# GpSimd's order at the start of a four-layer attention kernel: ones and query moves ahead of two memsets, register keys moved by SP, layer 0's weights in two loads

## The chip, the cores and the metric

The kernel runs on one core of a Trainium2 chip. The core has TensorE (PE, matmuls), VectorE (DVE), ScalarE (ACT), GpSimd (POOL) and SyncE (SP), each with its own instruction stream, and 16 DMA engines that serve the queues of SP, ACT and GpSimd. The metric is the device time of one execution in microseconds; lower is better.

## The reference

The input x has 16 x 16 places with 192 channels. Four attention layers are added to it one after the other, each on a group-normalised copy. Every layer has 12 heads of 16 channels over 256 places.

```python
x = x + L0(_gn(x))   # attention with relative position bias: q.Rh[row] + q.Rw[col]
x = x + L1(_gn(x))   # layer norm, rotary q and k, a bias per head, then a feed-forward block of 768
x = x + L2(_gn(x))   # 7 x 7 neighbourhood mask, and 16 register tokens as extra keys and values
x = x + L3(_gn(x))   # as L0
...
attn = softmax(q @ k.T * scale + bias);  out = (attn @ v) @ proj_w + proj_b
```

## The kernel before, in words

All activations stay in SBUF, channels on partitions, 96 channels in each of two chunks (NC = 2). Each engine has a stream written out by hand, with semaphores between them; nothing reorders it. `wait_ge` blocks the whole stream of its engine.

For the scores, queries and keys are stacked on partitions: QS[0] and QS[1] (layers 0 and 2, and 1 and 3) hold for each of the 12 heads 16 high query rows, 16 low query rows, the high rows again, and four blocks of bias or mask rows (ROW_HIGH, COL_HIGH, ROW_LOW, COL_LOW); KS holds the matching key rows, with 16 register columns in front and behind. A single 128-row matmul then gives a product of nearly full precision with the bias in it. Rows get into the stacks by small DMAs from SBUF to SBUF (`rows_of`), which is how this kernel moves data between partitions. The four first partitions of QS carry minus the maxima, and those of KS a one per head, loaded from `ones`.

A layer runs: group norm (`squares`, `stats_psum`, XN), projections, the split into high and low parts (QHL, KH, KL), in layers 0 and 3 the relative terms (ROWH, ROWL, COLH, COLL), the moves into QS and KS, and then on TensorE `for_maxima(l, h)` (L995), `turn_maxima` (L1009), `scores` (L1031), `values` (L1056) in a fixed interleaving, and `out_project` (L1066). The wait for the moves of the first heads stands ahead of head 0 ("q stack", "k stack", "first rows"); heads 4 and 8 wait for the second and third groups in layers 0 and 3, head 6 for the moves of the upper six heads in every layer ("later heads", "later keys").

Who moves what around the change: in layer 0 SP moves group 0's queries, keys and row terms, and the later row terms; GpSimd scales the key columns of w0 (L412), sets five backgrounds (VX, twice NM, ONESC, VR, L421), waits for the hot rows (the one-hot key rows, copied from HOT into KS by ACT, L538, and DVE, L843), loads `ones` (L425), and moves groups 1 and 2 of the queries (L455, L458), group 0's low row terms (L464) and all column terms (L441). Then it writes layer 1's bias rows (L485) and scales later weights. In layer 1 GpSimd moves the first six heads' low queries (L430) and high keys (L433), adds the rotated part to the second chunk of QF (L504), makes QL of it (L506), moves layer 2's register keys (L513, twelve moves of 6 KB) and layer 2's mask rows (L516, four of 192 KB). SP moves the rest (L329), ACT the high keys (L586).

`keep_warm(bank, n)` (L917) runs n matmuls on a tile of zeros whose result nobody reads. `project` (L935) and L1138, L1144 are projections; `loaded(pe, "w0")` is the wait for layer 0's weights, one load of 576 KB.

## Time and profile before

| | us |
|---|---|
| median of 3 runs | 158.56 |
| lowest, highest | 157.37, 159.72 |
| profiled execution, time | 159.08 |
| profiled execution, span from first to last instruction | 156.4 |
| TensorE busy | 141.6 (91% of the span) |
| VectorE busy | 91.1 (58%) |
| ScalarE busy | 70.7 (45%) |
| GpSimd busy | 53.1 (34%) |

Times in views are microseconds from the start of the span. The profiled execution is one more execution beside the three. TensorE's busy share holds warming matmuls too, and it is an average over stages: at the places of the change TensorE waits. Times of views with "issue" are times in which an engine waited for nothing that the profile shows.

### The profile page before, as it was taken

Reading aid. Unit: us, or ns where it says so; the run is one execution under the profiler, and the core shown is the slowest. Engines: PE = TensorE matmul, PEld = TensorE weight load, DVE = VectorE, ACT = ScalarE, POOL = GpSimd, SP = SyncE. Lnnn points to the kernel's source line nnn. Section 1 sums busy time; section 2 is a strip of 40 time slices with the busy share of each in tenths; the row PEclk is TensorE's granted clock in tenths of the full one; section 3 lists DMA queues with packets and bytes.
Section 4 is the critical chain, followed back from the end, with each engine's and each line's share of the span. In section 5 each row is a group of like instructions: output and inputs, shape, how many; then the busy total and the mean of one; then the engine's idle time right before and its main releaser. Section 6 shows DMA issues by size and latency. Waiting matters only on the chain.

```text
span 156.4 us, 2663 instructions
## 1 busy us (share of the span) xinstructions
PE 141.6 (91%) x920; PEld 94.2 (60%) x920; DVE 91.1 (58%) x239; ACT 70.7 (45%) x164; POOL 53.1 (34%) x94
## 2 busy tenths in 40 slices
PE   6989589999898958999999999968999999999992
PEld 2569366645457836755458865756666478676550
DVE  2775368736734988876541026666634845697462
ACT  4474127761233216682137713417571445167810
POOL 7689988840200289930000000720000047600000
PEclk9999999999999999999999999999999999999999
DMA  3907648999200156820000000450000017620001
GB/s 84 260 19 184 196 123 262 275 295 298 64 2 0 51 168 96 169 41 0 4 0 0 0 0 2 146 156 4 0 0 0 0 49 212 171 82 0 0 0 50
DMA packets 12508, 13.55 MB, mean 87 GB/s; under 512 B 4144, under 2 KB 10336, under 8 KB 12496
## 3 DMA queue, kind: packets, MB, share of 16 engines
q1 hardware_dynamic: 7792, 9.29, 21.0%
q0 software_dynamic: 3472, 3.01, 8.6%
q10 hardware_dynamic: 1232, 1.08, 2.4%
q8 instruction: 7, 0.11, 0.3%
q14 instruction: 5, 0.04, 0.1%
HBM read 6.82 MB, written 0.20 MB: 45 GB/s over the span
## 4 chain that ended last, share of the span: by engine, by line
PE 62%; DMA 9%; POOL 7%; ACT 7%; DVE 6%; issue 4%; SPq 3%; DVEq 0%; POOLq 0%; ACTq 0%
PE PC L1056 14%; PE RING L1031 9%; PE RING L917 4%; PE RING L995 4%; DMA KS<-KL 4%; PE PA L1066 4%; PE RING L1260 3%; DMA WQKV<-in_w 3%; PE PB L1066 3%; PE PB L995 2%; ACT PR L634 2%; DMA QS<-COLL 2%; SPq L329 2%; PE PA L1266 2%; PE PB L1266 1%
## 5 line engine op out<-in xcount | busy, mean ns | idle before, releaser
L634 ACT ACTIVATE PR<-RING 128x512 f32<-128x512 f32 (+1 forms) x48 | 25.7, 553 | 9.3 <-PE RING L1031 9.1
L917 PE MATMUL RING<-WARM 128*128 128x512 bf16 x84 | 24.7, 406 | 1.3 <-POOL WARM L388 1.3
L1056 PE MATMUL PC<-PR,VX 128*32 128x256 f32 (+1 forms) x192 | 23.6, 369 | 0.1
L827 DVE TENSOR_REDUCE NM<-RING 128x2 fp32r<-128x512 f32 (+1 forms) x32 | 20.1, 652 | 4.1 <-PE RING L995 3.9
L1031 PE MATMUL RING<-QS,KS 128*128 128x256 f32 (+1 forms) x96 | 20.2, 305 | 0.3 <-ACT QS L626 0.2
L1031 PEld LDWEIGHTS RING<-QS,KS 128*128 128x128 f32 x96 | 13.9, 188 | 7.7 <-issue 4.5
L626 ACT ACTIVATE QS<-PA 4x512 fp32r<-4x512 f32 (+1 forms) x20 | 10.6, 531 | 16.5 <-PE PA L1009 16.5
L430 POOL DMA_DIRECT2D QS<-QL x2 | 1.1, 550 | 43.0 <-DVE QL L778 31.0
L827 DVE TENSOR_REDUCE NM<-PB 128x2 fp32r<-128x512 f32 (+1 forms) x16 | 10.5, 654 | 5.6 <-PE PB L995 5.5
L1056 PEld LDWEIGHTS PC<-PR,VX 128*32 128x32 f32 x192 | 8.6, 109 | 8.4 <-ACT PR L634 1.8
L995 PE MATMUL RING<-KS,QS 128*128 128x256 f32 (+1 forms) x64 | 13.2, 298 | 0.0
L917 PEld LDWEIGHTS RING<-WARM 128*128 128x128 bf16 x84 | 8.3, 111 | 7.7 <-issue 1.6
L834 DVE STREAM_TRANSPOSE TURNED_U<-PC 128x256 f32<-128x256 f32 x12 | 5.4, 450 | 12.8 <-PE PC L1056 12.8
L995 PE MATMUL PB<-KS,QS 128*128 128x256 f32 (+1 forms) x32 | 7.3, 308 | 5.9 <-DMA QS<-COLL 2.7
L455 POOL DMA_DIRECT2D QS<-QHL x8 | 4.1, 516 | 24.8 <-ACT QHL L609 24.8
L995 PEld LDWEIGHTS RING<-KS,QS 128*128 128x128 f32 x64 | 9.4, 189 | 2.0 <-DVE NM L827 1.2
L995 PEld LDWEIGHTS PB<-KS,QS 128*128 128x128 f32 x32 | 5.0, 189 | 8.9 <-issue 7.2
L553 ACT ACTIVATE SQUARED<-X 96x256 f32<-96x256 f32 x8 | 3.3, 414 | 12.3 <-DVE X L890 7.9
L412 POOL TENSOR_SCALAR WQKV<-WQKV 96x384 f32<-96x384 f32 x4 | 5.3, 1324 | 9.7 <-DMA WQKV<-in_w 9.6
L1066 PE MATMUL PA<-O,WO 128*96 128x256 f32 x24 | 7.8, 405 | 0.0
L1066 PE MATMUL PB<-O,WO 128*96 128x256 f32 x24 | 7.1, 379 | 0.0
L485 POOL TENSOR_SCALAR QS<-HOT,ABS 128x256 fp32r<-128x256 f32 x12 | 6.7, 555 | 1.2
(189 smaller groups left out, 271.6 us busy)
## 6 DMA issues: line engine op xcount, KB each, us to landing
WQKV<-in_w SPq DMA_DIRECT2D x2, 576.0 KB, 8.5
WO<-in_wo SPq DMA_DIRECT2D x4, 288.0 KB, 8.8
W<-in_ff SPq DMA_DIRECT2D x2, 576.0 KB, 9.6
KS<-KH ACTq DMA_DIRECT2D x10, 96.0 KB, 3.1
WQKV<-in_w SPq DMA_DIRECT2D x2, 432.0 KB, 5.3
QS<-QHL POOLq DMA_DIRECT2D x12, 64.0 KB, 2.6
KS<-KL SPq DMA_DIRECT2D x8, 96.0 KB, 3.1
QS<-QH SPq DMA_DIRECT2D x8, 96.0 KB, 2.3
```

What stands on the lines that cost most here:

```text
L412: g.tensor_scalar(w[:, :, first:first + C], w[:, :, first:first + C], QK_SCALE, None, ALU.mult)\
L485: g.tensor_scalar(QS[1][:, h, :], HOT[:, :], ABS[:, 2, h:h + 1], ABS[:, 1, h:h + 1], ALU.mult, ALU.add).then_inc(sem("ab rows"), 1)
L626: A(QS[l % 2][0:GH, heads[0]:heads[-1] + 1, :], turn_bank(t)[0:GH, None, 0:T].to_broadcast([GH, len(heads), T]), ACT.Copy).then_inc(sem("m ...
L634: A(PR[:, h % NPR, 0:n], exponents(l, h)[:, 0:n], ACT.Exp).then_inc(sem("probs"), 1)
L827: V.tensor_reduce(NM[:, TURN_OF[h], :, h % GH], MAXIMA[h % 3][:, 0:2 * n_keys].rearrange("p (q k) -> p q k", q=2), AX.X, ALU.max, negate=T ...
L834: link(V.transpose(TURNED_U[:, :, :].rearrange("p b r -> p (b r)"), PC[g % 2][:, 0:T]))
L917: M(bank, WARM[:, 0:P], WARM[:, :], start=True, stop=True)
L995: ins = M(s[:, q * n_keys:(q + 1) * n_keys], QS[l % 2][:, h, q * P:(q + 1) * P], KS[:, h, keys], start=True, stop=True)
L1031: ins = M(half(s, l, k), KS[:, h, KEY0 + k * P:KEY0 + (k + 1) * P], QS[l % 2][:, h, reach(l, k)], start=True, stop=True)
L1056: ins = M(columns(h)[:, reach(l, k)], VX[:, k, h, :], half(PR[:, h % NPR, :], l, k), start=(k == 0 and l != 2), stop=(k == 1), skip_group_ ...
L1066: ins = M(y_psum(m), WO[l][:, g, m * CC:(m + 1) * CC], in_order(O[g][:, :]) if l in REL_LAYERS else O[g][:, :], start=(g == 0), stop=(g == ...
L1260: ins = M(s[:, i * T:(i + 1) * T], W1[:, k, c * P:(c + 1) * P], XN[:, k, :], start=(k == 0), stop=(k == NC - 1))
```

## The change

In words, part by part:

- GpSimd loads `ones` directly after the scaling of w0 and the wait for the hot rows, then sets VX and NM, and then starts on the query moves. ONESC and VR are set after layer 0's column terms.
- The hot rows are split 4 heads to ACT and 8 to DVE, before 6 and 6.
- Layer 0's weights come in two loads of 288 KB: query columns (w0q) ahead of vecs, and key and value columns where w0 stood. TensorE waits for w0q ahead of the query matmuls, and for w0 ahead of the keys. GpSimd's scaling waits for w0, now the second load.
- TensorE runs 5 warming matmuls in place of 7 ahead of layer 0's statistics, and none in place of 1 between the two.
- In layer 1 SP moves the low queries of the first six heads; GpSimd did. SP also moves the twelve register key pieces, behind its last move of layer 1, and waits for "kr parts" ahead of them.

GpSimd's stream at the start of layer 0, before. NM are zeros for the maxima, VX the values' tile, QHL the split queries.

```order
L412 TENSOR_SCALAR WQKV<-WQKV 96x2x192
L421 MEMSET VX 128x768
L421 MEMSET NM 128x192 x2
L421 MEMSET ONESC 96x96
L421 MEMSET VR 128x384
L425 DMA KS<-in_ones 4x12x272
L455 DMA QS<-QHL 16x4x256 x2
L458 DMA QS<-QHL 16x4x256
```

The same place now:

```order
L420 TENSOR_SCALAR WQKV<-WQKV 96x2x192
L427 DMA KS<-in_ones 4x12x272
L430 MEMSET VX 128x768
L430 MEMSET NM 128x192 x2
L466 DMA QS<-QHL 16x4x256 x2
L469 DMA QS<-QHL 16x4x256
L466 DMA QS<-QHL 16x4x256 x2
L469 DMA QS<-QHL 16x4x256
```

The load of ones moved ahead of the memsets, and two memsets left this place; they stand behind the last COLL move now.

GpSimd's stream in layer 1, before. QL, KH are low queries and high keys of a chunk, KRH and KRL the register keys.

```order
L430 DMA QS<-QL 16x6x256
L433 DMA KS<-KH 16x6x256
L504 TENSOR_TENSOR QF<-QF,RFq 48x256
L506 TENSOR_TENSOR QL<-QF,QH 96x256
L513 DMA KS<-KRH 16x6x16 x4
L513 DMA KS<-KRL 16x6x16 x2
L513 DMA KS<-KRH 16x6x16 x4
L513 DMA KS<-KRL 16x6x16 x2
L516 DMA QS<-in_mask 16x12x256 x4
```

The same place now:

```order
L444 DMA KS<-KH 16x6x256
L517 TENSOR_TENSOR QF<-QF,RFq 48x256
L519 TENSOR_TENSOR QL<-QF,QH 96x256
L523 DMA QS<-in_mask 16x12x256 x4
L459 MEMSET QS 4x3072
```

The four mask moves now stand directly behind QL, with no register keys ahead of them.

SP's stream in layer 1, as a difference (the rows without a sign are in both; in_w0q and the other loads stand far ahead of this):

```order
 L329 DMA QS<-QH 16x6x256 x2
+L329 DMA QS<-QL 16x6x256
 L329 DMA KS<-KL 16x6x256
 L329 DMA QS<-QH 16x6x256 x2
 L329 DMA QS<-QL 16x6x256
 L329 DMA KS<-KL 16x6x256
+L348 DMA KS<-KRH 16x6x16 x4
+L348 DMA KS<-KRL 16x6x16 x2
+L348 DMA KS<-KRH 16x6x16 x4
+L348 DMA KS<-KRL 16x6x16 x2
```

SP has one move more ahead of the first KL, and the twelve register moves behind the last.

```diff
@@ -67,7 +67,7 @@
     [f"bk{l}" for l in range(LAYERS)] + ["bkp"]
     + [f"{v}{l}" for l in range(LAYERS) for v in ("bq", "bo")] + ["bqp", "ln1g", "ln1b", "ln3g", "ln3b", "b2"])}
 
-HOT_HALF = NH // 2
+HOT_HALF = NH // 3
 SCALED = ("w0", "w2", "w1", "wp", "w3")
 
 def build(nc, a, out):
@@ -262,7 +262,7 @@
         def slot(*use):
             return RINGS[RING_OF[use[0]]][number[use] % 2]
 
-        loads = [("x", X, "xT"), ("gavg", GAVG, "gavg"), ("vecs", VECS, "vecs"), ("w0", WQKV[0], "w0"), ("hot", HOT, "hot"),
+        loads = [("x", X, "xT"), ("gavg", GAVG, "gavg"), ("w0q", WQKV[0][:, :, 0:Q2], "w0q"), ("vecs", VECS, "vecs"), ("w0", WQKV[0][:, :, Q2:Q2 + 2 * C], "w0"), ("hot", HOT, "hot"),
                  ("qbias", QBIAS, "qbias"), ("relt", RELT, "relt"), ("vb0", VB[:, 0, :], "vb0"), ("pcol", PCOL, "pcol"), ("abt", ABT, "abt")]
         later_loads = [
                  ("wo0", WO[0], "wo0"), ("vb", VB[:, 1:LAYERS, :], "vb"), ("w2", WQKV[2], "w2"), ("regt", REGT, "regt"), ("w1", WQKV[1], "w1"), ("wp", WP, "wp"),
@@ -282,11 +282,11 @@
         signals |= {"q psum": {0: NG, 1: NC, 2: NC, 3: NG}, "k psum": {l: NC for l in range(LAYERS)},
                     "turned": {1: 4 * NC}, "qf": {1: NC}, "kf": {1: NC},
                     "qh": {0: NG, 1: NC, 2: NC, 3: NG}, "ql": {0: NG, 1: NC, 2: NC, 3: NG},
-                    "q stack": {l: (5 if l in REL_LAYERS else 2) * 16 for l in range(LAYERS)},
+                    "q stack": {0: 5 * 16, 1: 3 * 16, 2: 2 * 16, 3: 5 * 16},
                     "k stack": {l: (3 if l in REL_LAYERS else 2) * 16 for l in range(LAYERS)},
                     "later heads": {l: (1 if l in REL_LAYERS else 4) * 16 for l in range(LAYERS)}}
         signals |= {"later keys": {l: 2 * 16 for l in range(LAYERS)},
-                    "first rows": {l: (4 if l in REL_LAYERS else 2) * 16 for l in range(LAYERS)}}
+                    "first rows": {0: 4 * 16, 1: 16, 2: 2 * 16, 3: 4 * 16}}
         signals |= {"x": {l: 3 * NC if l == 1 else NC for l in range(LAYERS)}, "sums": {0: 1}}
         signals |= {name: {l: count for l in REL_LAYERS} for name, count in {
             "rel psum": 4, "rel h": len(REL_PARTS), "rel l": len(REL_PARTS), "second heads": 4 * 16, "third heads": 4 * 16,
@@ -336,9 +336,17 @@
                         heads = slice(i * HPC, (i + 1) * HPC)
                         for block in (Q_HIGH, Q_AGAIN):
                             move("qh", rows_of(queries, block)[:, heads], QH[:, i, :], "later heads" if i else "q stack", i + 1)
-                        if i:
-                            move("ql", rows_of(queries, Q_LOW)[:, heads], QL[:, i, :], "later heads", i + 1)
+                        if i or l == 1:
+                            move("ql", rows_of(queries, Q_LOW)[:, heads], QL[:, i, :], "later heads" if i else "q stack", i + 1)
                         move("kl", rows_of(KS, Q_AGAIN, KEY0, REG1)[:, heads], KL[:, i, :], "later heads" if i else "k stack", i + 1)
+                    if l == 1:
+
+                        sync.wait_ge(sem("kr parts"), 2)
+                        for col in (0, REG1):
+                            for block, src in ((Q_HIGH, KRH), (Q_LOW, KRH), (Q_AGAIN, KRL)):
+                                for i in range(NC):
+                                    sync.dma_start(rows_of(KS, block, col, col + NREG)[:, i * HPC:(i + 1) * HPC].bitcast(F32), src[:, i, :].bitcast(F32))\
+                                        .then_inc(sem("kr stack"), 16)
                     continue
 
                 def move_group(signal, block, src, g, count):
@@ -415,20 +423,23 @@
 
             scale_keys("w0", WQKV[0], Q2)
 
-            for n, (tile, value) in enumerate((
-                    (VX[:, :, :, :], 1.0), (NM[:, 0:3].bitcast(F32), 0.0),
-                    (NM[:, 3:6].bitcast(F32), 0.0), (ONESC[:, :], 1.0 / C), (VR[:, :, :], 0.0))):
-                g.memset(tile, value).then_inc(sem("backgrounds"), 1)
-                pool.wait_ge(sem("backgrounds"), n + 1)
-
             pool.wait_ge(sem("hot rows"), 2)
             pool.dma_start(KS[0:GH, :, KEY0:REG1 + NREG], a["ones"]).then_inc(sem("one rows"), 16)
 
+            def background(n, tile, value):
+                g.memset(tile, value).then_inc(sem("backgrounds"), 1)
+                pool.wait_ge(sem("backgrounds"), n)
+
+            background(1, VX[:, :, :, :], 1.0)
+            background(2, NM[:, 0:3].bitcast(F32), 0.0)
+            background(3, NM[:, 3:6].bitcast(F32), 0.0)
+
             def move_first_rows(l):
 
-                pool.wait_ge(*upto("ql", l, 1))
-                pool.dma_start(rows_of(QS[l % 2], Q_LOW)[:, 0:HPC].bitcast(F32), QL[:, 0, :].bitcast(F32))\
-                    .then_inc(sem("first rows"), 16)
+                if l == 2:
+                    pool.wait_ge(*upto("ql", l, 1))
+                    pool.dma_start(rows_of(QS[l % 2], Q_LOW)[:, 0:HPC].bitcast(F32), QL[:, 0, :].bitcast(F32))\
+                        .then_inc(sem("first rows"), 16)
                 pool.wait_ge(*upto("kh", l, 1))
                 pool.dma_start(rows_of(KS, Q_LOW, KEY0, REG1)[:, 0:HPC].bitcast(F32), KH[:, 0, :].bitcast(F32))\
                     .then_inc(sem("first rows"), 16)
@@ -469,6 +480,8 @@
                     move_first_rows(2)
                 if l == 0:
 
+                    background(4, ONESC[:, :], 1.0 / C)
+                    background(5, VR[:, :, :], 0.0)
                     loaded(pool, "abt", "pcol", "hot")
                     g.tensor_scalar(ABH[:, :, :], ABT[:, :, :], 1.0, None, ALU.mult).then_inc(sem("ab cols"), 1)
                     pool.wait_ge(sem("ab cols"), 1)
@@ -506,12 +519,6 @@
                     g.tensor_tensor(QL[:, 1, :], QF[:, 1, :], QH[:, 1, :].bitcast(F32), ALU.subtract).then_inc(sem("ql"), 1)
 
                     pool.wait_ge(*upto("scores", 0, NH))
-                    pool.wait_ge(sem("kr parts"), 2)
-                    for col in (0, REG1):
-                        for block, src in ((Q_HIGH, KRH), (Q_LOW, KRH), (Q_AGAIN, KRL)):
-                            for i in range(NC):
-                                pool.dma_start(rows_of(KS, block, col, col + NREG)[:, i * HPC:(i + 1) * HPC], src[:, i, :])\
-                                    .then_inc(sem("kr stack"), 16)
                     for block in (ROW_HIGH, COL_HIGH, ROW_LOW, COL_LOW):
                         pool.dma_start(rows_of(QS[0], block), a["mask"][FREE + block:P:BLOCKS, None, :].to_broadcast([HD, NH, T]))\
                             .then_inc(sem("mask rows"), 16)
@@ -1108,7 +1115,7 @@
                 free = RINGS[0][0][:, :]
                 if l:
                     pe.wait_ge(*upto("probs", l - 1, max(AFTER_MAXIMA) + 1))
-                keep_warm(free, (7, 3, 3, 3)[l])
+                keep_warm(free, (5, 3, 3, 3)[l])
                 if l == 0:
                     loaded(pe, "gavg")
                 for i in range(NC):
@@ -1118,7 +1125,7 @@
                         pe.wait_ge(*upto("x", l - 1, signals["x"][l - 1] - NC + i + 1))
                     pe.wait_ge(*upto("squares", l, i + 1))
                     M(stats_psum(i), GAVG[:, :], SUMS[:, i, :], start=True, stop=True).then_inc(sem("gstats"), 1)
-                    if i == 0:
+                    if i == 0 and l:
                         keep_warm(free, 1)
                 keep_warm(free, 2 if l == 1 else 7)
                 if l == 1:
@@ -1130,7 +1137,7 @@
                     layer_norm(1, free, *ready)
                     register_keys()
                     ready = upto("ni", 1, NC)
-                loaded(pe, f"w{l}")
+                loaded(pe, f"w{l}" if l else "w0q")
                 if l in REL_LAYERS:
                     for k in range(NC):
                         chunk_ready(*ready, k)
@@ -1143,6 +1150,7 @@
                     for k in range(NC):
                         ins = M(thirds, WQKV[l][:, k, 2 * P:3 * P], by_parity(XN[:, k, :]), start=(k == 0), stop=(k == NC - 1))
                     ins.then_inc(sem("q psum"), 1)
+                    loaded(pe, f"w{l}")
                     pe.wait_ge(sem("k scaled"), 2 + SCALED.index(f"w{l}"))
                     project(chunk_psum("k", l, 0), WQKV[l], Q2, *ready).then_inc(sem("k psum"), 1)
                 else:
@@ -1378,6 +1386,7 @@
     for l in range(LAYERS):
         arrays[f"w{l}"] = chunks(wqkv[l])
         arrays[f"wo{l}"] = by_quadrant(wo[l])
+    arrays["w0q"], arrays["w0"] = arrays["w0"][:, :, 0:Q2], arrays["w0"][:, :, Q2:]
     return {name: np.ascontiguousarray(v, dtype=f32) for name, v in arrays.items()}
 
 def kernel(**inputs):
```

## Rows read from the trace of the kernel before

**Rows 1.** The page, chain of work that ended last, shares of the span by engine.

```profile
PE 62%; DMA 9%; POOL 7%; ACT 7%; DVE 6%; issue 4%; SPq 3%; DVEq 0%; POOLq 0%; ACTq 0%
```

**Rows 2.** The chain, pieces in order of time, 0 to 24: start, length, what.

```profile
1.65 0.43 SPq L322
...
7.17 1.81 POOL WQKV L412
...
10.45 0.17 POOL ONESC L421
...
10.68 0.43 POOL VR L421
11.11 0.30 issue
11.41 0.79 POOL KS L425
...
16.74 3.26 DMA QS<-COLL
```

**Rows 3.** Timeline of TensorE, 0 to 22.5: start, busy, line, operation, count.

```profile
1.31 3.17 PE L917 MATMUL RING<-WARM 128*128 128x512 bf16 x7 [1.31 <-POOL WARM L388]
...
5.12 1.88 PE L917 MATMUL RING<-WARM 128*128 128x512 bf16 x7
7.06 0.70 PE L1138 MATMUL PA<-XN,WQKV 96*128 96x256 f32 x2
...
20.23 0.48 PE L995 MATMUL PB<-KS,QS 128*128 128x256 f32 x2 [2.42 <-DMA QS<-COLL]
```

**Rows 4.** Timeline of DVE and ACT, 6.9 to 9.

```profile
7.03 0.41 DVE L720 TENSOR_SCALAR XN<-X,GM,GT 96x256 f32<-96x256 f32 x1
...
7.34 1.48 ACT L538 ACTIVATE KS<-HOT 128x1536 fp32r<-128x1536 f32 x1 [1.19 <-DMA HOT<-in_hot]
...
7.41 1.20 DVE L843 CAST KS<-HOT 128x1536 fp32r<-128x1536 f32 x1
```

**Rows 5.** The chain, pieces in order of time, 54 to 62.

```profile
58.18 3.01 DMA KS<-KL
```

**Rows 6.** Timeline of all engines, 50 to 72, the rows of layer 1's moves.

```profile
53.91 0.56 SPq L329 DMA_DIRECT2D KS<-KL  x1
...
53.95 0.56 POOL L430 DMA_DIRECT2D QS<-QL  x1 [11.96 <-DVE QL L772]
54.32 0.47 DVE L763 SCALAR_TENSOR_TENSOR RFq<-PC,VECS,ROPE 48x256 f32<-48x256 f32 x1
...
55.06 0.74 POOL L504 TENSOR_TENSOR QF<-QF,RFq 48x256 f32<-48x256 f32 x1
...
56.99 2.04 POOL L513 DMA_DIRECT2D KS<-KRH  x4
...
57.21 0.47 PE L995 MATMUL PB<-KS,QS 128*128 128x256 f32 x2 [1.63 <-DMA KS<-KH]
...
61.28 0.47 PE L995 MATMUL PB<-KS,QS 128*128 128x256 f32 x2 [0.57 <-DMA KS<-KL]
...
63.05 2.17 POOL L516 DMA_DIRECT2D QS<-in_mask  x4
```

**Rows 7.** DMA queues (q1 SP, q10 ACT, q0 GpSimd): 58.2 to 60.2; 60.2 to 61.4; 63.6 to 64.6; 65.6 to 66.6.

```profile
q1 hardware_dynamic: 324, 0.29, 50.6%
q0 software_dynamic: 381, 0.02, 29.0%
q10 hardware_dynamic: 165, 0.14, 23.6%
...
q1 hardware_dynamic: 12, 0.01, 1.5%
...
GB/s 0 41 54 19 29 44 23 18 5 0 0 0 0 0 0 0 0 0 0 0 0 0 0 0 0 0 0 0 0 82 861 123 123 205 205 287 246 287 410 205
...
q0 software_dynamic: 323, 0.31, 133.7%
```

## The prediction

> **What bounds the kernel now.** I read the chain of work that ended last first, then its pieces in order of time over the two places that the change touches, then the timeline there. TensorE carries 62% of the chain, DMA 9% and GpSimd 7% [rows 1]. The change touches almost nothing on TensorE, so what it can move lies in the small shares: the start of layer 0, where the chain runs over GpSimd and a transfer, and the start of layer 1, where it runs over SP and a transfer. Both are places where TensorE stands still and waits for data.
>
> Layer 0: the chain is the load of w0, then GpSimd alone: key scaling from 7.17 to 8.98, five memsets, the load of ones at 11.41, the query moves from 11.41 + 0.79 = 12.20, and at last the first group's low column terms, issued at 16.74 and landed 3.26 later [rows 2]. The first maximum matmul starts at 20.23 after 2.42 us of waiting for that transfer [rows 3]. GpSimd issues one move right behind the other from 11.41 on, so its queue is the limit, and what goes from in front of it comes off the start of the attention one for one, down to about 17.8, where TensorE's own work ends (20.23 less 2.42).
>
> Layer 1: head 0 starts at 57.21 after 1.63 us of waiting for GpSimd's key move, but this is given back: the chain does not end there. Head 6 starts at 61.28 and waits 0.57 us for the last key-low move, which SP issued at 58.18 and which took 3.01 [rows 5, 6]. So head 6 is the wait that sets layer 1, and head 0 is not.
>
> **Part 1, GpSimd in layer 0: two memsets leave the queue's front.** ONESC costs 0.17 and VR 0.43; with a step of 0.05 behind each (10.45 + 0.17 to 10.68) that is 0.70. Between the last memset and the first DMA lie 0.30 of issue [rows 2]. In the new order a compute instruction stands before a DMA twice (key scaling before ones, NM before the query moves). If the 0.30 is paid twice the gain is 0.70 - 0.25 = 0.45; if the step costs 0.05 both times, it is 0.70 + 0.25 = 0.95. The row that exists is 0.30 for a memset before a DMA, so one 0.30 and something between for the other: I take 0.6. The two memsets come back after the column terms, in front of the bias rows of layer 1. That costs the bias rows 0.70 - 0.6, about 0.1 us, well ahead of layer 1 in time: nothing.
>
> **Part 2, the new gate in front of the ones.** Its DMA, and behind it everything that GpSimd does, waits for both halves of the hot rows. Before, ACT took 6 heads in 1.48 (7.34 to 8.82) and DVE 6 in 1.20 (7.41 to 8.61) [rows 4], both under the key scaling. Now DVE has 8 heads: 1.20 x 8/6 = 1.60, so it ends at 9.01, 0.03 after the key scaling. Cost 0.05. This cover is now gone: each 0.1 us that HOT lands later costs GpSimd 0.1. HOT is issued one SP issue later (0.43 [rows 2], about 0.47 with the step to the next); if the landing follows in full, GpSimd loses 0.45 of its 0.6. I take no delay, because HOT landed close behind w0 (ACT started on it at 7.34, GpSimd on w0 at 7.17) and the same bytes stand before it as before: the engines were busy with w0 then, not waiting for an issue. For ACT the smaller half is a gain: 1.48 x 4/6 = 1.0, the table's high part RELH, next on ACT, starts some 0.4 earlier, and with it the high and low query parts, about 0.3. SP's moves start 0.3 earlier by that; they are not last at 20.23.
>
> **Part 3, w0 in two loads.** The queries' half takes the place of vecs in the issue order, so its bytes can start 0.47 earlier, and the rest is issued 0.47 later than w0 was. The query matmuls started at 7.06 [rows 3], as w0 landed, but their second chunk needs XN, which DVE finished at 7.03 + 0.41 = 7.44 [rows 4]; they gain some 0.4, and their reader, ACT, is busy with hot rows until then, so it lies under part 2. For the end only the second half counts, since key scaling waits for it. Landing bounds: 0.4 earlier to 0.47 later. I take 0.
>
> **Part 4, three warming matmuls fewer.** Seven take 3.17 from 1.31, 453 ns each, so the seventh ends at 4.48 [rows 3]; five end near 3.6, and the sums, not the warming, then set the start. The statistics start about 0.25 earlier, and XN with them. It is off GpSimd's path: 0.
>
> Layer 0 in sum: -0.6 + 0.05 + 0 + 0 = **-0.55**, bounds -1.3 (0.95 and the early landing) and +0.3 (0.45, and both loads late).
>
> **Part 5, layer 1's first low query move goes from GpSimd to SP.** GpSimd loses one issue of 0.56 at 53.95, so the key move behind it can go about 0.5 earlier, and head 0 gains about 0.4. SP takes it in between the high queries and the key-low move of 53.91, which it hardly delays, since SP waits there for DVE anyway. What counts for head 6 is the add on QF at 55.06: it also needs the rotated part that DVE has ready at 54.32 + 0.47 = 54.79 [rows 6]. So it starts at about 54.85: 0.2 earlier, no more. QH, SP's four moves and the key-low move follow 0.2 earlier, issued at 57.98.
>
> **Part 6, the register keys go to SP, and the mask rows come forward.** In the kernel before GpSimd spent 56.99 to 63.05 on twelve small moves, and only then issued the four mask moves [rows 6]. Now the twelve stand on SP behind the last key-low move, where SP has nothing to do until layer 2: twelve times 0.6 is 7 us from 58.6, hidden. But GpSimd now issues the four mask moves at about 57.0, into the transfers on which head 6 waits. No row shows this; two rows bound it. In the two us from 58.2, SP's queue moved 0.29 MB and ACT's 0.14, with only 0.02 of GpSimd's between, and the key-low move took 3.01 [rows 5, 7]. The mask alone fills the engines, 0.31 MB per us [rows 7], and it is 4 x 192 KB. Its first bytes came 1.3 after its first issue (63.05, [rows 6]), in slice 30 of 40 from 63.6, at 64.3 [rows 7]; here that is 58.2 or just after. If the three queues take turns, then from 58.2 on SP's remaining 0.27 MB (0.29 + 0.01 before, less what moves in the 0.2 us of the earlier start) get 0.10 per us while ACT has its last 0.12 (1.2 us), then half of 0.31: 0.15 / 0.155 = 1.0. The last bytes move near 60.4; before it was about 60.2, after which SP's queue had only 0.01 MB [rows 7]. So taking turns costs 0.0 to 0.3. If the transfers go in order of issue, some 0.58 MB of mask stand in front of the last key-low move; at 0.31 from about 57.4 on, 1.3 after SP's first issue, (0.48 + 0.58 + 0.10) / 0.31 = 3.7 gives 61.1 and, with the 1.0 between last bytes (60.2) and landing (61.19), 62.1 to 62.4: 0.9 to 1.2 later than 61.19. Below zero: if the mask cost nothing and the twelve small moves (29% of the engines' time in these 2 us) were gone, the landing would be 0.5 earlier. I take turns, because the row shows all three queues moving in the same 2 us, none waiting for the other: head 6 at 61.5, **+0.2** instead of the -0.2 that part 5 alone would give. From head 6 on TensorE works in order, so the layer shifts by it.
>
> The Trainium skill, "DMA: Bandwidth & Descriptors", section "Queues, rings and completion order", says that each engine goes round robin between queues, a whole packet of descriptors at a time. This speaks against the order-of-issue price and for +0.2; by the same page's rule that all issuers share the same 16 engines the mask is not free either. The row with three queues active agrees.
>
> **Sum.** -0.55 + 0.2 = -0.35, with rounding -0.4. The profiled execution took 159.08 (span 156.4, 2.7 around it), which makes 158.7. It was 0.5 above the median of the three runs, so against the median of 158.56 the forecast is **158.2**. The three runs spread over 157.37 to 159.72; 2% is 3.2 us, about what a measurement of this kernel can tell from no change.
>
> **The rivals.**
> A, slower: the mask moves delay head 6. It decides as soon as the key-low move lands more than 0.55 later than in the profile before, after 61.75. In order of issue it is +1.0, up to +1.4 if all of the mask goes first: 158.56 - 0.55 + 1.0 = 159.0, at most 159.4. For it: the engines are at nine tenths there already. Against: the queues take turns in the row. Chance 0.20.
> B, layer 0 gains nothing: HOT or the second half of w0 lands an SP issue later, hot rows end at 9.5, GpSimd gains 0.15, and layer 1 gives +0.2: 158.6. That is also what the change would be if it did not do what it says, since its query moves would then leave when they did. For it: 288 KB in shorter rows, one issue more in front. Chance 0.12.
> C, both ends good: 0.95 in layer 0, and no collision, -0.5 in layer 1: 158.56 - 1.45 = 157.1. For it: the small moves that leave the critical 2 us. Against: 0.30 has been seen. Chance 0.15.
> D, TensorE's clock: the first seven warming matmuls took 453 ns each, the later seven 269 [rows 3], the step from 1.2 to 2.4 GHz. With three fewer and a pause of some 0.5 us before the sums it may rise later. The query matmuls, of which a pair takes 0.70 or less [rows 3], then take up to twice as long: six pairs, between 0 and some 3 us. GpSimd's queue covers part of it; I take +1.0 on the start of layer 0 in place of the -0.55, with layer 1's 0.2: 159.8. Against: in the profile longer pauses (2.42 us before 20.23) leave the clock granted full. Chance 0.05. The Trainium skill, "TensorE: Matmul & The Clock Gate", section on the HAM clock gate, says that the array starts throttled and that activity releases it; the rows agree with the first half.
>
> **How the numbers follow.** The forecast, 158.2 with its own range of 157.6 to 158.7, has 0.48; A 0.20, C 0.15, B 0.12, D 0.05. From C, less the spread of a median of few runs, to the upper end of A; D lies above it: 156.9 to 159.5. No case leaves the 2% band; what is left for either side is what I have not seen: 0.04 faster, 0.92 same, 0.04 slower.
>
> **What the changed profile would show.** Right: GpSimd's first query move at 11.6 instead of 12.20, the first maximum at 19.7, its wait still for COLL; head 6 of layer 1 waiting longer than 0.57 for the key-low move, which takes 3.3 to 3.6. Wrong: the ones after 9.5 (B), a landing over 4 us (A), query matmuls of 12% to 100% longer (D), a head 6 without a wait (C). The forecast is also wrong if the start of layer 0 moves earlier and head 4 or 6 there takes up the wait, behind the later groups' moves, or if layer 2's start moves though nothing there was changed.

## The result, and the profile after

| | before | after |
|---|---|---|
| median, us | 158.86 (4 runs, 157.37 to 159.72) | 163.44 (4 runs, 162.85 to 165.16) |
| ratio, 95% interval | | 1.032, 1.020 to 1.043 |
| profiled execution, us (its span) | 159.08 (156.4) | 165.16 (163.4) |

The change makes the kernel 3% slower, 4.6 us. The forecast was 158.2, with a range of 156.9 to 159.5. Medians here and below hold all runs; the ratios leave out runs over 1.5% above the fastest of their kernel, which leaves e4 without a ratio. Lines of the code are some 7 further down after the change: L995 is now L1002, L1138 is L1145, L1031 is L1038.

The page of the changed kernel, the chain by engine and by line, is the first hint: TensorE's share is down from 62% [rows 1] and DMA's is up from 9%, and key-low moves alone have 6%.

```profile
PE 59%; DMA 12%; DVE 8%; POOL 7%; ACT 6%; issue 4%; SPq 3%; DVEq 0%; POOLq 0%; ACTq 0%
PE PC L1063 14%; PE RING L1038 9%; DMA KS<-KL 6%; PE RING L1002 4%; PE PA L1073 4%; PE RING L924 4%; DMA QS<-COLL 3%; PE RING L1268 3%; DMA WQKV<-in_w 3%; PE PB L1002 3%; PE PB L1073 3%; SPq L329 2%; PE PA L1274 2%; PE PB L1274 2%; DVE NM L834 2%
```

The chain of the changed kernel in order of time over layer 1's start (start, length, what) shows which one:

```profile
58.33 6.03 DMA KS<-KL
```

It was issued at 58.33, before at 58.18, and took 6.03 us instead of 3.01 [rows 5]. Head 6 starts at 64.45 instead of 61.28. The timeline of the changed kernel there has both sides of it: GpSimd's mask moves are issued from 1.4 us ahead of SP's last key-low move on, and TensorE waits 3.95 where it waited 0.57 [rows 6].

```profile
55.03 0.72 POOL L517 TENSOR_TENSOR QF<-QF,RFq 48x256 f32<-48x256 f32 x1 [0.25 <-DVE RFq L770]
...
56.95 2.18 POOL L523 DMA_DIRECT2D QS<-in_mask  x4
...
57.00 0.47 PE L1002 MATMUL PB<-KS,QS 128*128 128x256 f32 x2 [1.26 <-DMA KS<-KL]
...
57.47 0.82 SPq L329 DMA_DIRECT2D QS<-QL  x1
...
58.33 0.65 SPq L329 DMA_DIRECT2D KS<-KL  x1
...
59.03 2.52 SPq L348 DMA_DIRECT2D KS<-KRH  x4
...
64.45 0.77 PE L1002 MATMUL PB<-KS,QS 128*128 128x256 f32 x2 [3.95 <-DMA KS<-KL]
...
65.90 1.07 PE L1063 MATMUL PC<-PR,VX 128*32 128x256 f32 x4
```

The DMA view of the changed kernel, packets, MB and share of 16 engines by queue, once for 58.2 to 60.2 and once for 60.2 to 62.2, says who had the engines. In the first two us SP's queue (q1) got 0.12 MB where it had 0.29 before [rows 7], and GpSimd's (q0) got twice that; in the next two, 2.7 times that.

```profile
q0 software_dynamic: 253, 0.24, 53.0%
q10 hardware_dynamic: 147, 0.13, 26.0%
q1 hardware_dynamic: 137, 0.12, 21.5%
...
q0 software_dynamic: 421, 0.40, 84.9%
q1 hardware_dynamic: 172, 0.15, 32.3%
q10 hardware_dynamic: 76, 0.06, 11.3%
```

Head 6 is 3.17 us late, but layer 1's end (the first sums of the next norm, 76.12 before and 81.97 after) is 5.85 late. The windows view of the changed kernel (length, busy time and count by engine, then the granted clock, DMA share, GB/s) has the other 2.7: TensorE stands still for the pause, and for 6.8 us behind it runs at about half clock (0.52 granted), that is at 1.2 GHz. Four value matmuls then take 1.07 us, against 0.63 at full clock. In the kernel before, the clock is full from 58 to 76.

```profile
58.00:61.30 3.30, 2.45 (x17) 1.85 (x15) 3.19 (x6) 1.84 (x4) 3.30 (x4) 1.00 0.99 249
61.30:64.20 2.90, 0.00 (x0) 0.00 (x0) 0.00 (x0) 0.00 (x0) 0.43 (x1) 0.95 0.99 171
64.20:71.00 6.80, 6.55 (x28) 4.42 (x29) 2.77 (x5) 2.31 (x4) 0.00 (x0) 0.52 0.07 8
71.00:76.00 5.00, 5.00 (x42) 2.98 (x40) 4.09 (x14) 4.25 (x9) 0.00 (x0) 1.00 0.00 0
```

Layer 0 gave nothing in this execution: the first maximum stands at 20.71, before at 20.23. The chain of the changed kernel there: the second w0 load lands at 7.58, the step behind the scaling is 0.42, the step behind NM 0.29, and the query moves leave at 12.58, not at 11.6 (before: 12.20).

```profile
3.02 4.56 DMA WQKV<-in_w
...
7.73 1.95 POOL WQKV L420
9.68 0.42 issue
10.10 0.79 POOL KS L427
...
12.28 0.29 issue
12.58 1.03 POOL QS L466 x2
...
17.12 3.35 DMA QS<-COLL
20.47 0.24 issue
20.71 0.48 PE PB L1002 x2
```

A last loss stands where nothing was changed: in layer 3, head 4 waits 1.29 us, where before it did not wait. The view names DVE's maxima, but those that head 4 needs were done; what came last is a move of ROWL by SP, issued at 140.2, which took 4.1 us to land, when no such move took over 3.0 before. Timeline of the changed kernel, then its view of ROWL moves from 120 us on:

```profile
144.38 0.47 PE L1002 MATMUL RING<-KS,QS 128*128 128x256 f32 x2 [1.29 <-DVE NM L834]
```

```profile
DMA to landing us min/median/max: 1.8/2.3/4.1
```

### The profile page after: what moved, and what is told of

Same layout as the page of the kernel before. It is cut to its first block, busy times and chain, and to the rows that moved or that the text cites. A ratio compares the mean times of both kernels' runs of the same rounds, so it can differ in the third digit from the quotient of the medians.

```text
span 163.4 us, 2651 instructions
## 1 busy us (share of the span) xinstructions
PE 144.6 (89%) x909; PEld 96.2 (59%) x917; DVE 91.4 (56%) x239; ACT 70.5 (43%) x164; POOL 46.6 (29%) x81
## 4 chain that ended last, share of the span: by engine, by line
PE 59%; DMA 12%; DVE 8%; POOL 7%; ACT 6%; issue 4%; SPq 3%; DVEq 0%; POOLq 0%; ACTq 0%
PE PC L1063 14%; PE RING L1038 9%; DMA KS<-KL 6%; PE RING L1002 4%; PE PA L1073 4%; PE RING L924 4%; DMA QS<-COLL 3%; PE RING L1268 3%; DMA WQKV<-in_w 3%; PE PB L1002 3%; PE PB L1073 3%; SPq L329 2%; PE PA L1274 2%; PE PB L1274 2%; DVE NM L834 2%
## 5 line engine op out<-in xcount | busy, mean ns | idle before, releaser
L1063 PE MATMUL PC<-PR,VX 128*32 128x256 f32 (+1 forms) x192 | 24.5, 379 | 0.1
L924 PE MATMUL RING<-WARM 128*128 128x512 bf16 x74 | 22.8, 420 | 1.6 <-POOL WARM L396 1.3
L1038 PE MATMUL RING<-QS,KS 128*128 128x256 f32 (+1 forms) x96 | 20.7, 311 | 0.4 <-ACT QS L633 0.2
L1038 PEld LDWEIGHTS RING<-QS,KS 128*128 128x128 f32 x96 | 14.4, 195 | 8.2 <-issue 5.1
L1002 PE MATMUL PB<-KS,QS 128*128 128x256 f32 (+1 forms) x32 | 7.8, 328 | 8.7 <-DMA KS<-KL 6.2
L1002 PE MATMUL RING<-KS,QS 128*128 128x256 f32 (+1 forms) x64 | 13.9, 310 | 1.3 <-DVE NM L834 1.3
L441 POOL DMA_DIRECT2D QS<-QL x1 | 0.5, 536 | 43.1 <-DVE QL L785 43.1
L1002 PEld LDWEIGHTS PB<-KS,QS 128*128 128x128 f32 x32 | 5.4, 206 | 11.7 <-issue 10.7
L1002 PEld LDWEIGHTS RING<-KS,QS 128*128 128x128 f32 x64 | 10.1, 202 | 3.5 <-DVE NM L834 3.1
L420 POOL TENSOR_SCALAR WQKV<-WQKV 96x384 f32<-96x384 f32 x4 | 5.4, 1358 | 11.8 <-DMA WQKV<-in_w 11.6
```

The costliest lines, as they stand in the source:

```text
L420: g.tensor_scalar(w[:, :, first:first + C], w[:, :, first:first + C], QK_SCALE, None, ALU.mult)\
L924: M(bank, WARM[:, 0:P], WARM[:, :], start=True, stop=True)
L1002: ins = M(s[:, q * n_keys:(q + 1) * n_keys], QS[l % 2][:, h, q * P:(q + 1) * P], KS[:, h, keys], start=True, stop=True)
L1038: ins = M(half(s, l, k), KS[:, h, KEY0 + k * P:KEY0 + (k + 1) * P], QS[l % 2][:, h, reach(l, k)], start=True, stop=True)
L1063: ins = M(columns(h)[:, reach(l, k)], VX[:, k, h, :], half(PR[:, h % NPR, :], l, k), start=(k == 0 and l != 2), stop=(k == 1), skip_group_ ...
```

## The experiments

The kernel before, run beside them each time, had medians of 158.67 (e1 to e4), 158.64 (e5 to e9), 159.02 (e10 to e13) and 158.98 (e14 to e17). Each run's profile is one execution.

**e1, the masks held back.**

```diff
+                    pool.wait_ge(*upto("later heads", 1, 4 * 16))
                     for block in (ROW_HIGH, COL_HIGH, ROW_LOW, COL_LOW):
```

> The changed kernel, but GpSimd waits for the upper six heads' moves of layer 1 (later heads) before it issues the four mask moves; all else as changed. Theory M (the mask moves in front of head 6 cost the time: 3.95 us of waiting for the last key-low move against 0.57, and behind the pause a lower TensorE clock): the key-low move takes about 3 us again, head 6 waits under 0.6 us, the clock stays granted, and the time is 158.5 to 160. Theory S (the start of layer 0 costs it: one load more, three warming matmuls fewer): unchanged within 1 us of the changed kernel, 162.5 to 164.

Measured: 159.47, ratio 1.005 (0.998 to 1.012). Timeline of e1: the key-low move issued at 58.64 landed in 2.2 us, head 6 started at 60.93 without a wait, and head 0 within 0.4 of where it was. This one wait takes back 3.8 of the 4.6 us (the 0.8 left lies within the interval), so the mask's place is the cause. The twelve register moves are still on SP here: they are not. With them gone from GpSimd's queue the landing is even 0.8 shorter than the 3.01 of before, which e10 and e11, where they stay on it, have too (3.0).

```profile
57.41 0.47 PE L1003 MATMUL PB<-KS,QS 128*128 128x256 f32 x2 [1.37 <-DMA KS<-KL]
...
58.64 0.61 SPq L329 DMA_DIRECT2D KS<-KL  x1
...
61.42 2.17 POOL L524 DMA_DIRECT2D QS<-in_mask  x4 [4.14 <-PE RING L1039]
```

**e2, only the twelve register moves put on SP,** in the kernel before; the mask rows come forward by that.

```diff
+                        sync.wait_ge(sem("kr parts"), 2)
...
+                                    sync.dma_start(rows_of(KS, block, col, col + NREG)[:, i * HPC:(i + 1) * HPC].bitcast(F32), src[:, i, :].bitcast(F32))\
...
-                    pool.wait_ge(sem("kr parts"), 2)
...
-                                pool.dma_start(rows_of(KS, block, col, col + NREG)[:, i * HPC:(i + 1) * HPC], src[:, i, :])\
```

> The kernel before, and of the change only the twelve register key moves put on SP, so that GpSimd's mask moves come forward by 6 us. Theory M: the key-low move takes 5 to 6 us, head 6 waits 3 to 4 us, and the time is 3 to 4.5 us over the kernel before, 162 to 163. Theory S: no change, 158 to 159.5.

Measured: 162.77, ratio 1.022 (1.013 to 1.030). The key-low move took 4.85 us, and head 6 waited for it:

```profile
58.02 0.47 PE L997 MATMUL PB<-KS,QS 128*128 128x256 f32 x2 [1.60 <-DMA KS<-KH]
63.95 0.47 PE L997 MATMUL PB<-KS,QS 128*128 128x256 f32 x2 [2.44 <-DMA KS<-KL]
```

This part alone brings most of the loss. In its profiled execution (163.78) the clock was at half for 3.4 us here too, from 65.4 on.

**e3 and e4, the start of layer 0 undone:** the warming matmuls back to 7 and 1 (e3), w0 in one load again (e4), each in the changed kernel.

```diff
-                keep_warm(free, (5, 3, 3, 3)[l])
+                keep_warm(free, (7, 3, 3, 3)[l])
-                    if i == 0 and l:
+                    if i == 0:
```

```diff
-        loads = [..., ("w0q", WQKV[0][:, :, 0:Q2], "w0q"), ("vecs", VECS, "vecs"), ("w0", WQKV[0][:, :, Q2:Q2 + 2 * C], "w0"), ...
+        loads = [..., ("vecs", VECS, "vecs"), ("w0", WQKV[0], "w0"), ...
```

> The changed kernel with the three warming matmuls of layer 0 put back (7 and 1). Theory M: the start of layer 0 gives back at most 0.5 us, 163 to 163.5, and head 6 of layer 1 waits as in the changed kernel. Theory S: if the clock that rose at 9.3 us in place of 5.8 is what costs, 159 to 161.

> The changed kernel with layer 0's weights in one load again, in its old place in the order. Theory M: key scaling starts at 7.2 in place of 7.7, the first maximum of layer 0 about 0.5 us earlier, 162.7 to 163.4. Theory S: if the second load is what costs, 159 to 161.

Measured: e3 165.5, ratio 1.038 (1.029 to 1.047); e4 165.59. The first matmul of full-clock length starts at 5.0 in e3, as before at 5.8, and at 9.3 in the changed kernel (read from the matmuls' lengths; the granted clock of the windows view is 1.00 there all the way). The time is not better, so neither brings the loss; the key-low move took 5.5 and 5.8 us in them. A few tenths stay possible: in e3's trace the clock was at 0.66 from 21 to 26, where the changed kernel had 1.00, which would hide a small gain, and e12 below undoes both at once and comes out 0.7% under e1, inside both intervals. In e4 w0 was issued at 2.11 and landed in 4.92, at 7.03, as in the kernel before, 0.55 earlier than in the changed kernel. That is one pair of traces: with two loads the key scaling began at 7.15 (e3) to 7.96 in seven kernels, with one load at 7.12 to 7.34 in eleven, so the second load costs it some 0.4 us in the mean and nothing in e3.

**e5, the clock held up in the pause:** 16 warming matmuls ahead of head 6 of layer 1.

```diff
+                if h == HPC and l == 1:
+                    keep_warm(s[:, :], 16)
```

> The changed kernel with 16 warming matmuls (some 3.5 us at full clock) on TensorE ahead of head 6's wait in layer 1. It parts the wait from what follows it. Theory W+C (the wait of about 4 us costs about 3, and the lower clock behind it another 2 to 2.5): the wait for the key-low move stays near 6 us from issue, the clock stays granted behind it, and the time is 1.5 to 2.5 us below the changed kernel, near 161 to 162. Theory W (the wait alone costs, the clock is small): within 0.7 us of the changed kernel.

Measured: 162.56, ratio 1.022 (1.017 to 1.028). Timeline and windows of e5: head 6 is as late as in the changed kernel (64.36), but the clock behind it stays full.

```profile
60.70 3.63 PE L924 MATMUL PB<-WARM 128*128 128x512 bf16 x16
64.36 0.50 PE L1004 MATMUL PB<-KS,QS 128*128 128x256 f32 x2
...
65.20 0.63 PE L1065 MATMUL PC<-PR,VX 128*32 128x256 f32 x4
```

```profile
64.30:71.00 6.70, 6.66 (x51) 4.54 (x52) 4.83 (x9) 4.19 (x9) 0.00 (x0) 1.00 0.06 6
```

e5 is 3.9 over the kernel before, the changed kernel 4.6: the clock is some 0.7 of the medians (1% by the ratios, 2.7 us in the profiled execution; it differs between executions), and with the 0.8 that e1 keeps, the wait itself is 3.1. That the clock fell for the pause is shown; what it costs in the median is not settled, since the intervals of e5 and of the changed kernel overlap.

**e6 and e9, whose bytes they are and on which queue.** Both start from e1. They add four plain loads of the same mask rows into an unused tile DUM, 768 KB; e6 on GpSimd, where the change had the mask moves, e9 on SP directly behind its last key-low move.

```diff
+                        pool.dma_start(rows_of(DUM, block), a["mask"][FREE + block:P:BLOCKS, None, :].to_broadcast([HD, NH, T]))\
```

```diff
+                            sync.dma_start(rows_of(DUM, block), a["mask"][FREE + block:P:BLOCKS, None, :].to_broadcast([HD, NH, T]))\
```

> The mask moves wait for the upper heads' moves as in e1, and at their early place GpSimd issues four plain loads of the same rows, size and shape into a scratch tile that nothing reads (extra work). The mask moves convert float32 to the matmul's rounded float32 on the way, these do not. Theory B (bytes and packets of GpSimd's queue delay the key-low move): it takes 5 to 6 us as in the changed kernel, time 162.5 to 165. Theory K (the conversion is what makes the collision dear): the key-low move takes 3.3 to 4 us, time 159.5 to 161.

> As e6, but SP issues the four plain loads, directly behind its last key-low move, so that they stand in the same queue and behind it, at nearly the same time (from 59). Theory Q (the order in one queue protects what is ahead): the key-low move takes 3 to 3.3 us, head 6 waits under 0.6 us, time as e1, 158.5 to 160. Theory T (all traffic in flight shares the engines alike): the key-low move takes over 4 us, time over 161.

Measured: e6 165.68, ratio 1.046 (1.037 to 1.054), key-low 5.83 us, head 6 waiting 3.64: bytes for an unused tile delay it as the mask rows do. e9 157.81, ratio 0.993 (0.989 to 0.997), key-low 2.2 us, no wait of head 6. The same bytes, 0.7 us behind the key-low move instead of 1.4 ahead of it, cost nothing. Two things differ between e6 and e9, the queue and the moment of issue, and no run parts them: large loads on SP ahead of the key-low move, or on GpSimd's queue right behind it, were not tried. The DMA view of e9, 58 to 62 (issues: KB each, median us to landing):

```profile
q1 hardware_dynamic: 846, 0.78, 60.3%
q10 hardware_dynamic: 175, 0.15, 11.9%
...
DUM<-in_mask SPq DMA_DIRECT2D x4, 192.0 KB, 3.4
...
KS<-KL SPq DMA_DIRECT2D x1, 96.0 KB, 2.2
```

**e7, half of the dose:** two of the four mask moves ahead, two behind the wait of e1.

```diff
+                        if block == ROW_LOW:
+                            pool.wait_ge(*upto("later heads", 1, 4 * 16))
```

> Two of the four mask moves (384 KB) go at the early place, two behind the upper heads' moves. Theory B in proportion: the key-low move takes about 4.4 us in place of 3 or 6, head 6 waits 1.5 to 2.5, and the clock mostly stays; time 160 to 161.5. Theory F (a move behind them waits for whatever was issued before, so the first ones decide): the same as with all four, over 162.5.

Measured: 161.11, ratio 1.012 (1.005 to 1.019). Key-low 4.32 us (2.2 with none of the mask, 6.03 with all of it); head 6 at 62.97, after 2.10 of waiting, and no fall of the clock in its trace. Landing against bytes is near proportional: some 2 us of landing for each 384 KB ahead, of which TensorE feels what is over some 2.3 (3.01 and 0.57 of waiting before, 4.32 and 2.10 here).

```profile
58.56 4.32 DMA KS<-KL
62.97 0.47 PE PB L1004 x2
```

**e10 and e11, the rest of the change by itself.** e10 is the kernel before with GpSimd's new order in layer 0 only; e11 adds the first low query move on SP in layer 1, with the register moves on GpSimd, and the mask behind them, as before.

```diff
-HOT_HALF = NH // 2
+HOT_HALF = NH // 3
+            background(1, VX[:, :, :, :], 1.0)    # behind the ones; ONESC and VR behind COLL
-                        if i:
+                        if i or l == 1:                # e11 only
```

> The kernel before with only GpSimd's new order in layer 0: the hot rows split 4 to 8, ones behind the key scaling, VX and NM, then the query moves, and ONESC and VR behind the column terms. One w0 load, the warming matmuls, and all of layer 1 as before. If the layer 0 part failed through the second load and SP's longer issues, this alone gives 0.3 to 0.5: query moves near 11.8, first maximum near 19.8, 158.0 to 158.4 against 158.6 before. If the issue step in front of a transfer is paid twice and eats it, nothing: first maximum at 20.0 to 20.3, 158.5 to 158.8. Head 6 of layer 1 waits 0.5 to 0.6, as before.

> The one before, plus the move of the first low query part of layer 1 on SP; the twelve register moves stay on GpSimd in front of the masks. Part 5 of the prediction says 0.2 less than the run with the order alone, by the wait of head 6 (0.57 to some 0.4): 157.8 to 158.2. Rival: the move stands on SP's queue in front of the key-low move and delays it by its own issue, so nothing, or 0.1 to 0.3 more. The key-low move should take about 3, not 4 to 6, since no mask bytes stand before it.

Measured: e10 159.2, ratio 0.998 (0.992 to 1.004); e11 158.92, ratio 1.002 (0.998 to 1.007). Neither part changes the time beyond the intervals. The chain of e10:

```profile
7.18 2.06 POOL WQKV L412
9.24 0.41 issue
9.64 0.79 POOL KS L419
...
11.84 0.29 issue
12.13 1.03 POOL QS L457 x2
```

Two memsets (0.70) are gone, but the step in front of a DMA is paid twice, 0.41 and 0.29 for 0.30, and the scaling next to DVE's longer copy took 2.06 for 1.81 [rows 2]: 12.13 against 12.20. The first maximum of e10 still came at 19.53, 0.70 earlier than before, because the COLL move behind it landed in 2.60 instead of 3.26. That landing varies by itself: e12, e14, e15 and e16 are the same program up to there and have 3.73, 2.64, 3.76 and 3.52. A few tenths won on GpSimd are smaller than this spread. In e11 the add on QF starts 0.96 us behind the start of DVE's last QF step and in e10 1.14, so 0.18 is gained, as part 5 says; but the low query move of SP ahead of the key-low move takes 0.82 instead of 0.61, and the key-low move stands 4.26 us behind that DVE step in both (52.95 to 57.21, 54.12 to 58.38).

**e12 and e13, the best of the parts:** e1 with the warming and the one load of before (e12), and with DMA_WARM, the warming matmuls in the pauses ahead of head 0, raised (e13).

```diff
-DMA_WARM = (2, 3, 3, 2)
+DMA_WARM = (10, 7, 8, 2)
```

> The changed kernel with the mask moves held back behind the later heads of layer 1 (as in the first of these runs), the old warming (7 and 1) and one w0 load. What is left of the change: GpSimd's order, QL and the register moves on SP. If the warming and the load explain the 0.8 that the first run stayed above the kernel before, it comes to 157.6 to 158.6. If those 0.8 are the mask's later place or the extra work on SP, it stays at 159 to 159.5. Key-low landing 2 to 2.5, no wait of head 6.

> The same with more warming matmuls while TensorE waits for the moves ahead of head 0 (10, 7, 8 and 2 instead of 2, 3, 3 and 2). If the granted clock falls behind the pause ahead of head 0 of layer 0 (half at 21 to 25 in runs so far) because TensorE stood still there, it stays full now, and the time falls by 0.5 to 1.5 against the run without. If the warming reaches past the landing of the moves, head 0 starts later by up to 1 us and it is a wash.

Measured: e12 159.11, ratio 0.998 (0.992 to 1.004); e13 158.25, ratio 0.999 (0.995 to 1.003). e12 has no wait of head 6, yet gains nothing on the kernel before: head 4 of layer 3 waits, as in the changed kernel and in e1 (timeline of e12; then its ROWL moves from 120 us on):

```profile
138.71 0.47 PE L1003 MATMUL RING<-KS,QS 128*128 128x256 f32 x2 [1.08 <-DVE NM L835]
```

```profile
DMA to landing us min/median/max: 2.0/2.8/3.7
```

e13 kept the clock full in 11 of 12 runs. The kernel before on that chip had it full (0.997 or more) in 10 of 35, with a mean of 157.69, and a mean of 159.29 in the 24 at 0.986 to 0.989. But e13's own 11 average 158.15, so part of that was lost again; by what is not shown.

**e14 to e17, the late move in layer 3.** In every kernel with twelve register moves on SP up to here but e9 and e13 one ROWL move of layer 3 took 3.3 us or more (changed kernel 4.1, e1 4.2, e2 4.0, e3 3.4, e4 3.9, e5 3.3, e6 3.9, e7 3.8, e12 3.7), in before, e10 and e11 none over 3.0, nor in e9, with four more DMAs on SP (2.7). So four (e14) or eight (e15) copies of 6 KB to an unused tile, behind the register moves in e12; e9's four large loads in e12 (e16); and e14 with DMA_WARM of (10, 3, 3, 2) (e17).

```diff
+                        for n in range(4):             # e15: 8
+                            sync.dma_start(rows_of(DUM, Q_HIGH, n * NREG, (n + 1) * NREG)[:, 0:HPC]..., KRH[:, 0, :]...)
```

> e12 (mask late, old warming, one load) with four small copies of 6 KB to an unused tile on SP's queue behind the twelve register moves; result unused. If the number of DMAs on SP's queue sets which one lands late, the slow one leaves the place that head 4 of layer 3 waits for: ROWL at most 3.0 instead of 3.7, no wait of head 4 (e12: 1.08), 0.7 to 1.2 us less than e12, 157.5 to 158.3 against 159 before on the chip of e12. If the number does not matter, it stays as e12: a landing of 3.5 or more and a wait near 1.

> The same with eight small copies. If a periodic event of SP's queue is what is seen, eight put it at another DMA again; no wait of head 4, or a late move at another place (a group of third heads, layer 3's first heads, or a later load), so a time within 0.5 of e14. If more DMAs only give more delay, a longer wait than in e12.

> e12 with e9's four unused loads of 192 KB on SP between its last key-low move and the register moves. The number of DMAs is that of e14. If the number counts, this is as e14 within 0.4, without a wait of head 4 in layer 3, whatever the bytes; e9's result (0.7% faster than the kernel before) repeats. If e9 was chance, it comes out at e12's time or the time before, with a wait of head 4 near 1.

> e14 with ten instead of two warming matmuls in the pause ahead of head 0 of layer 0 alone. In e13 such warming in four layers kept TensorE's clock full in 11 of 12 runs, but full-clock runs were 0.5 us over those of before. With layer 0's alone the clock should stay full in most runs and those 0.5 should go if they came from the other layers' warming: 157 to 157.7, 1% below the kernel before. If the clock falls behind head 0 of layer 1 or 2 instead, it is as e14.

| | median | ratio | longest ROWL | wait of head 4, layer 3 |
|---|---|---|---|---|
| e14 | 158.78 | 0.996 (0.990 to 1.001) | 2.9 | none |
| e15 | 158.03 | 0.994 (0.988 to 0.999) | 3.0 | none |
| e16 | 158.7 | 0.998 (0.992 to 1.005) | 3.0 | none |
| e17 | 157.66 | 0.993 (0.989 to 0.998) | 3.0 | none |

Four, eight and four large ones all take the wait away, and 6 KB copies do it as well as 192 KB. That speaks for the number of DMAs on the queue and against their bytes; with one trace for each kernel, and with e13 against it, it is not shown. Whether the late one then only stands at another DMA, where nobody waits, is not known. The gain on e12 in the ratio is only 0.2% to 0.4% (0.0% in e16), within the intervals, so what the wait is worth in the whole is not settled.

e17 is, with e9, the best version: below the kernel before by 0.7% in the ratio, and more so in the median of all runs (157.66 to 158.98), since its clock was full in 12 of 12 runs (mean 157.52), where the kernel before had it full in 14 of 35 (157.88) and was at 159.50 in the 18 at 0.986 to 0.989. e14, which differs from e17 by the eight matmuls alone, had it full in 3 of 12. So most of the gain in the median (158.78 to 157.66) is the warming's and not the change's, and warming alone in the kernel before was not tried. Windows of e17, 10 to 21 and 21 to 26, have the clock; in e16, with two warming matmuls in the same pause of 3 us, the same 5 us had 0.66 (in e14's one trace 1.00).

```profile
10.00:21.00 11.00, 10.31 (x87) 7.49 (x86) 5.80 (x14) 3.53 (x8) 10.27 (x23) 1.00 0.64 174
21.00:26.00 5.00, 4.96 (x38) 3.65 (x38) 4.86 (x9) 3.53 (x8) 4.14 (x9) 1.00 0.56 169
```

## Why the prediction was wrong

**Part 6 is the step that failed.** It put the mask's price on head 6 at 0.0 to 0.3 by "taking turns" and at 0.9 to 1.2 by "order of issue", and took the first. The place, the mechanism and the released wait were right; rival A, "the mask moves delay head 6", is what happened, given 0.20 and a ceiling of 159.4. Measured: the landing is at 64.36 instead of 61.19, +3.2, more than twice A's highest price, 1.4. The mask's first bytes came at 58.2, as forecast. Two numbers in the working are wrong. The queues don't share evenly: SP's got a quarter of the bytes in the two us behind its last issue (0.12 of 0.49 MB) and in the next two (0.15 of 0.61), GpSimd's half and then two thirds. And the rate of 0.31 MB per us, taken from a stretch in which the mask moved alone [rows 7], was not there with three queues: 0.25 in the first two us. The row on which I chose, three queues moving in the same two us, held GpSimd's moves of 6 KB only, 0.02 MB in all [rows 7]; it could not show how large ones are served. e1, e2, e6 and e7 show the cause from four sides, and e9 that the same bytes are free behind the key-low move on its own queue.

The Trainium skill, "DMA: Bandwidth & Descriptors", section "Queues, rings and completion order", says that an engine serves its queues round robin, a whole packet of descriptors at a time. I read that as equal thirds. The page speaks of turns and not of shares; equal shares were my reading, and the measurement contradicts that reading. The trace has 253, 137 and 147 entries for GpSimd's, SP's and ACT's queues, and then 421, 172 and 76. Nor do turns of so many entries fit both traces: in e6 GpSimd's entries are larger (3.2 KB in the mean against 1.0), and the two us at the same distance behind the last key-low move's issue (61.5 to 63.5) have as many entries of SP as of GpSimd, and yet 3.5 times the bytes for GpSimd. Its DMA view:

```profile
q0 software_dynamic: 132, 0.42, 69.3%
q1 hardware_dynamic: 130, 0.12, 19.2%
```

What sets the shares is not shown.

**What I gave no place: the clock behind the new pause.** Rival D looked for a late clock only in layer 0. A longer wait at head 6 made a pause of nearly four us, and the clock fell to half behind it; e5 puts that at 0.7 us of the 4.6 by the medians. D's own mechanism did happen (query matmuls 7.63 1.06 for a pair, before 7.06 0.70 [rows 3]; matmuls of full-clock length only from 9.3), but the first maximum waited for COLL all the same (2.04 us), so GpSimd's queue hid it; e3 has the early clock and no better time. Against D stood that the clock stays full behind the pause ahead of head 0 of layer 0. That was one execution: in nine of the 18 profiled ones, e1 and e10 among them, it fell to half behind that pause.

**Parts 1 to 4: -0.55 was forecast; the first maximum came 0.5 later.** The step in front of a DMA was 0.42 and 0.29, not 0.30 and something between. That is 0.41 more than before, where I had 0.1 (0.70 less 0.6). Part 2's 1.60 for 8 heads on DVE was 1.25 (up to 1.52 in the other runs), and HOT landed later, which it took at nothing: DVE's copy began at 8.06 and not 7.41. Both stayed under the scaling, which was as late, and which took 1.95 for 1.81. Part 3's zero was wrong: SP's issue of w0q took 0.71 for 0.43 and the next three 0.58 to 0.59, so w0 was issued at 3.02, not at 2.6, and landed 0.55 later. That is rival B ("layer 0 gains nothing"), and e10 shows that GpSimd's queue gains nothing without the second load either. Layer 1 begins only some 0.15 late (DVE's first step on QF, 50.45 against 50.30).

**Part 5** was right on the add (0.25 of waiting for RFq, starting at 55.03) and wrong in the sum: 0.18 won there, 0.21 lost on SP's issue (e11).

**The end, layer 3:** the text named layer 2 as a place whose shift would prove it wrong, and not layer 3. Twelve moves put "on SP, hidden" may not have been free: in nine kernels that have them one of SP's later DMAs landed late, in none that leaves them on GpSimd.

## What to carry to other kernels

When a change lets an engine issue a large transfer earlier, look up what small transfer somebody waits for in the following five us, and on which queue it is: behind it in the same queue 768 KB cost nothing, ahead of it on GpSimd's queue 3 us. A row in which queues share the engines bounds only transfers of the size that it holds. Price the pause as well as the wait: stalls of TensorE of 2.4 to 4 us at head 6 were followed by 3.4 to 6.8 us at half clock in five traces, one of 2.1 us (e7) by none, and warming matmuls in the stall kept the clock full (e5).

## What was not expected of the hardware

- SP's queue beside GpSimd's with 192 KB moves: 0.12 MB against 0.24, then 0.15 against 0.40, in two us each.
- In layer 3, one of SP's 32 KB moves landed in 3.3 to 4.2 us instead of at most 3.0 in traces where the queue had had 12 to 14 more DMAs, and not so with 17, 18 or 21 more. e13, with 13 more, had 3.0 and no such wait; the pattern is therefore not strict. What it is in the queue stays open.
- The granted clock explains much of the spread from run to run: on the last chip the kernel before took 157.88 us in the mean at full clock (14 runs) and 159.50 at 0.986 to 0.989 (18 runs). With ten warming matmuls in layer 0's pause it was full in 12 of 12 runs, with two in 3 of 12 (e17, e14).
- In layer 0 GpSimd took 0.29 to 0.42 us between a compute instruction and the DMA behind it, both times, in the changed kernel, e10, e11, e12 and e13 alike.
- The same DVE copy of 2048 elements a partition, beside GpSimd's scaling, took 1.25 us in the changed kernel and up to 1.52 in others (e15); 1536 elements took 1.20 [rows 4].
